# Means and roots of six routing passes made in one batch in the second attention's lead-out

## The reference

```python
x = x + _L1_ffn_ref(_layernorm(x, axis=-1), ...)

for _ in range(LOOPS):                      # LOOPS = 2
    z_norm = _rmsnorm(z, norm_w)            # mean of squares + 1e-6
    logits = z_norm @ router_w              # 8 experts
    scores = softmax(logits)
    topk_vals, topk_idx = top_k(scores, 2)  # weights normed to sum 1
    mixed = sum over experts e of cw[:, e] * ((silu(z_norm @ w1[e]) * (z_norm @ w3[e])) @ w2[e])
    z = z + mixed
```

## Time and profile before

| what | value |
|---|---|
| median of 3 runs | 2263.12 us (2262.07 to 2265.07) |
| the profiled execution | 2267.05 us, its span 2265.3 us |
| instructions | 47236 |
| mean granted clock of PE | 0.966 of full speed |

### The profile page before, as it was taken

One profiled execution on the slowest core, in us unless ns is written; L12 is line 12 of the kernel. 1 busy time (PEld: TensorE's weight loads), 2 busy tenths in 40 slices (PEclk: granted clock), 3 DMA queues, 4 the chain that ended last, 5 costly groups with the idle time before them and its releaser, 6 DMA issues. The chain is left out here.

```text
span 2265.3 us, 47236 instructions
## 1 busy us (share of the span) xinstructions
PE 2000.4 (88%) x14589; PEld 958.0 (42%) x14589; DVE 1849.5 (82%) x5293; ACT 1465.1 (65%) x3369; POOL 1235.4 (55%) x1708
## 2 busy tenths in 40 slices
PE   5999999999988999899999999985788999999992
PEld 1222222222222466444444444442455666666662
DVE  8999999999999576788888888885878787767555
ACT  1788888888888533477777777772445655565551
POOL 6343343343321012567677777744566777777776
PEclk9999999999999999799999999995889999999996
DMA  7355345345432002242333433312233444444544
GB/s 187 104 125 139 114 113 144 111 108 140 130 104 84 3 1 56 58 108 65 95 77 86 86 82 91 75 42 75 79 103 98 122 120 120 123 126 124 145 134 111
DMA packets 224626, 226.94 MB, mean 100 GB/s; under 512 B 34048, under 2 KB 187520, under 8 KB 224384
## 3 DMA queue, kind: packets, MB, share of 16 engines
q1 hardware_dynamic: 152432, 164.62, 28.0%
q0 software_dynamic: 16384, 33.59, 5.1%
q10 hardware_dynamic: 55568, 25.71, 3.9%
HBM read 96.48 MB, written 125.76 MB: 98 GB/s over the span
## 5 line engine op out<-in xcount | busy, mean ns | idle before, releaser
L899 ACT ACTIVATE big<-mid_ps 128x512 f32<-128x512 f32 (+2 forms) x1792 | 914.1, 568 | 268.5 <-PE mid_ps L778 260.7
L984 DVE TENSOR_REDUCE mid_nmax<-mid_ps 128x1 f32<-128x512 f32 (+2 forms) x1280 | 776.8, 658 | 61.3 <-PE mid_ps L757 35.5
L757 PE MATMUL mid_ps<-KT,QT 48*128 48x512 bf16 (+3 forms) x2048 | 605.1, 351 | 68.3 <-DVE mid_nmax L984 49.7
L778 PE MATMUL mid_ps<-QT,KT 64*128 64x512 bf16 (+3 forms) x2048 | 564.4, 347 | 2.7 <-ACT big L899 2.7
L794 PE MATMUL mid_ps<-big,vv 128*32 128x512 f32 (+3 forms) x4096 | 467.8, 530 | 16.7 <-POOL big L1115 12.8
L757 PEld LDWEIGHTS mid_ps<-KT,QT 48*128 48x128 bf16 x2048 | 159.1, 94 | 586.3 <-DVE mid_nmax L984 397.8
L981 DVE CUSTOM_DVE_ANT_0 big<-mid_ps,mask 128x512 bf16<-128x512 f32 (+1 forms) x512 | 304.6, 620 | 70.1 <-PE mid_ps L757 65.2
L1628 PE MATMUL moe_ps<-big,moe_xinT 128*128 x638 | 337.7, 612 | 0.0
L1773 POOL DMA_INDIRECT moe_yg<-rows_out,moe_gat_idx x256 | 251.6, 983 | 80.8 <-issue 65.8
L1759 POOL DMA_INDIRECT rows_in<-moe_xn,moe_scat_idx x240 | 236.6, 986 | 108.0 <-issue 58.9
L1690 ACT ACTIVATE moe_xinT<-moe_ps,norm_w 128x128 f32<-128x128 f32 x319 | 116.6, 366 | 226.3 <-PE moe_ps L1640 154.6
(11 more groups left out here) (328 smaller groups left out, 3047.5 us busy)
## 6 DMA issues: line engine op xcount, KB each, us to landing
l_spread<-mid_slots SPq DMA_DIRECT2D x128, 384.0 KB, 5.3
rows_in<-mid_blank SPq DMA_DIRECT2D x64, 512.0 KB, 3.7
QT<-l_spread SPq DMA_DIRECT2D x128, 192.0 KB, 4.3
KT<-l_spread SPq DMA_DIRECT2D x128, 192.0 KB, 5.3
moe_xin<-rows_in SPq DMA_DIRECT2D x319, 64.0 KB
rows_out<-moe_y ACTq DMA_DIRECT2D x319, 64.0 KB
x<-in_L_attn_x_dram SPq DMA_DIRECT2D x8, 512.0 KB, 6.5
QT<-mid_mrows SPq DMA_DIRECT2D x256, 6.0 KB
```

Of the source, the lines that this page charges most:

```text
L757: mm = pe.matmul(ps[:, bank, n_keys * a:n_keys * (a + 1)], QT[rows, par, pair, i * P:(i + 1) * P], KT[rows, par, pair, 0:n_keys], start=Tr ...
L778: mm = pe.matmul(ps[:, bank, m * a:m * (a + 1)], KT[rows, own, pair, i * P:(i + 1) * P], QT[rows, own, pair, SEQ - m:SEQ], start=True, sto ...
L899: act.activation(weights_of(r, i, heads), ps[:, ring(S2, n - 2, k), 0:widths[i] * len(heads)], ACT.Exp, scale=scale).then_inc(exp_done, 1)
L984: dve.tensor_reduce(to, of, X_AXIS, ALU.max, negate=True).then_inc(s1_used, 1)
```

## The change

`Lead.ahead` is new. It makes the statistics of x for passes 1 to 6 (48 tiles of rows, x tiles 8 to 55), their means, the first roots (`roots`) and the second roots (`scales`) in arrays of 48 columns, in four parts: part 0 (40 bn_stats) at the end of (0, 0), part 1 (8 bn_stats and the moments) at (1, 15) ahead of the wait for the router products, part 2 (first root and what leads to the second) at (2, 5), part 3 (second root) at (4, 0). It uses the centering arrays of the second attention as scratch. In the experts' block passes 1 to 6 then skip s = 0 to 3, 5 to 8 on DVE and read means, roots and scales. The passes' table is changed: `begin` of passes 2, 3, 5, 6, 7 and 8, and `length` of passes 1 to 6 is 10 and no longer 14. POOL's due times follow from them.

```diff
--- before.py
+++ after.py
@@ -408,6 +408,7 @@
         self.xn, self.z = sb("xn", [P, IT, DIM], F32), sb("z", [P, IT, DIM], F32)
         self.sel = sb("sel", [P, 2, IT, EXPERTS], F32)
         self.at, self.weight, self.scat = sb("at", [P, 2, IT], F32), sb("weight", [P, 2, IT], F32), sb("scat", [P, 2, IT], I32)
+        self.means, self.roots, self.scales = (sb(k, [P, 6 * IT], F32) for k in ("means", "roots", "scales"))
         self.run_sum, self.region, self.falling = (sb(k, [P, EXPERTS], F32) for k in ("run_sum", "region", "falling"))
         self.upper, self.ones = sb("upper", [P, P], BF16), sb("ones", [P, P], BF16)
         self.const, self.chain = sem("const"), sem("chain")
@@ -418,8 +419,9 @@
         self.sel_ready, self.k_made = sem("sel_ready"), sem("k_made")
         self.scattered = [sem(f"scattered{a}") for a in range(3)]
 
-    def place(self, big, ps, zeroed):
-
+    def place(self, big, ps, zeroed, center):
+
+        self.center = center
 
         self.zT, self.zeroed = big[:, self.ZT:self.ZT + IT * P], zeroed
         self.psT = [ps[:, a, :] for a in range(2)]
@@ -488,6 +490,36 @@
             act.activation(m["pr"], m["sh"], ACT.Exp).then_inc(self.exp_ready, 1)
             act.wait_ge(self.second_ready, 1)
             act.activation(m["e2"], m["second"], ACT.Exp).then_inc(self.e2_ready, 1)
+
+    def ahead(self, dve, part, x_added):
+
+        c, n = self.linked, 6 * IT
+        stats = self.center["stats"]
+        var, diff, tmp = (self.center[k][:, 0:n] for k in ("var", "diff", "nmean"))
+        means, roots, scales = self.means[:, :], self.roots[:, :], self.scales[:, :]
+        even, odd = stats[:, 0:n, 1], stats[:, 0:n, 4]
+        if part < 2:
+            if part == 0:
+                dve.wait_ge(x_added, BATCHES - 2)
+            for t in range(0, 5 * IT) if part == 0 else range(5 * IT, n):
+                last = dve.bn_stats(stats[:, t, :], self.x[:, IT + t, :])
+            c.link(last)
+        if part == 1:
+            dve.tensor_tensor(means, even, odd, ALU.add)
+            dve.tensor_tensor(var, stats[:, 0:n, 2], stats[:, 0:n, 5], ALU.add)
+            c.link(dve.tensor_tensor(diff, even, odd, ALU.subtract))
+            dve.tensor_scalar(means, means, 0.5, None, ALU.mult)
+            dve.tensor_scalar(var, var, 1.0 / DIM, None, ALU.mult)
+            c.link(dve.scalar_tensor_tensor(diff, diff, 0.25, diff, ALU.mult, ALU.mult))
+            c.link(dve.tensor_tensor(var, var, diff, ALU.add))
+            c.link(dve.tensor_scalar(diff, var, 1e-5, None, ALU.add))
+        if part == 2:
+            c.link(rsqrt(c, roots, diff, tmp))
+            c.link(dve.tensor_tensor(var, var, roots, ALU.mult))
+            c.link(dve.tensor_tensor(var, var, roots, ALU.mult))
+            c.link(dve.tensor_scalar(var, var, 1e-6, None, ALU.add))
+        if part == 3:
+            c.link(rsqrt(c, scales, var, tmp))
 
     def vector(self, dve, off, u, x_added):
 
@@ -532,8 +564,14 @@
             c.link(dve.tensor_scalar(var, var, 1e-6, None, ALU.add))
             c.link(rsqrt(c, rstd, var, tmp))
             dve.tensor_tensor(self.xn[:, :, :], self.z[:, :, :], each_row(rstd), ALU.mult).then_inc(self.xn_ready, 1)
+            self.ahead(dve, 0, x_added)
+        if (off, u) == (2, 5):
+            self.ahead(dve, 2, x_added)
+        if (off, u) == (4, 0):
+            self.ahead(dve, 3, x_added)
         if (off, u) == (1, 15):
             c = self.linked
+            self.ahead(dve, 1, x_added)
             dve.wait_ge(self.r_made, 1)
             c.link(dve.tensor_tensor(lg, self.psR, over(rstd), ALU.mult))
             c.link(dve.tensor_reduce(m["mx"], lg, X_AXIS, ALU.max))
@@ -1263,7 +1301,7 @@
         shared["PT"] = big
         for k, rows in (("ffn_xnT", lead_pass.xn), ("ffn_sg", lead_pass.z)):
             shared[k] = rows[:, :, :].rearrange("p (a t) d -> p a (t d)", a=2)
-        lead_pass.place(big, ps, zeroed)
+        lead_pass.place(big, ps, zeroed, center)
 
         spare, at = shared["PT"], 2 * 4 * P * TILES * (TILES + 1) // 2
         for k, n in (("qk", 2 * SEQ), ("squares", 2 * SEQ), ("gvar", P), ("grs", P), ("gtmp", P), ("aoT", SEQ), ("proj", SEQ),
@@ -1401,14 +1439,14 @@
     HT, MOST = IT * max(sizes), max(tiles_in)
     unit_of = [max(u for u in range(UNITS) if first_of[u] <= k) for k in range(LOOPS * GROUPS)]
     EARLY, PER_TILE = 2, 0.5
-    begin = {2: 0, 3: 10, 4: 22, 5: 36, 6: 49, 7: 62, 8: 78, 9: 97, 10: 117, 11: 137, 12: 158, 13: 179, 14: 200, 15: 224,
+    begin = {2: -1, 3: 8, 4: 22, 5: 34, 6: 46, 7: 60, 8: 76, 9: 97, 10: 117, 11: 137, 12: 158, 13: 179, 14: 200, 15: 224,
              16: 256, 17: 270, 18: 286, 19: 308, 20: 325}
     transfers = ("s1 s2 s3 g8 s4 s5 s6 g9 s7 g10 s8 g11 s9 g12 s10 g13 s11 g14 s12 g15 s13 g16 s14 g17 s15 g18 "
                  "g19 g20 g21 g22 g23").split()
 
     def length(k):
 
-        return 14 if k < GROUPS else 20 if k < LOOPS * GROUPS else 8
+        return 10 if k < GROUPS - 1 else 14 if k < GROUPS else 20 if k < LOOPS * GROUPS else 8
 
     def sides(n):
 
@@ -1869,6 +1907,12 @@
                         moments()
                         c.link(dve.tensor_tensor(ms[:, :], mean[:, :], mean[:, :], ALU.mult))
                         c.link(dve.scalar_tensor_tensor(var[:, :], var[:, :], 1e-6, ms[:, :], ALU.add, ALU.add))
+                elif 1 <= k < GROUPS - 1:
+                    own = slice(IT * (k - 1), IT * k)
+                    if s == 4:
+                        c.link(dve.tensor_tensor(zs, xs, each_row(lead.means[:, own]), ALU.subtract))
+                        dve.tensor_tensor(zs, zs, each_row(lead.roots[:, own]), ALU.mult).then_inc(z_ready, 1)
+                        dve.wait_ge(z_ready, k + 1)
                 else:
                     if s == 0:
                         c.link(bn(xs))
@@ -1892,18 +1936,20 @@
                 if not routes(k):
                     return
 
-                if s == 6:
+                made = 1 <= k < GROUPS - 1
+                scale = lead.scales[:, IT * (k - 1):IT * k] if made else rstd[:, :]
+                if s == 6 and not made:
                     rsqrt_seed(c, rstd[:, :], var[:, :])
                     cubic_root(c, rstd[:, :], var[:, :], tmp[:, :])
-                if s == 7:
+                if s == 7 and not made:
                     cubic_step(c, rstd[:, :], tmp[:, :])
-                if s == 8:
+                if s == 8 and not made:
                     c.link(newton(c, rstd[:, :], var[:, :], tmp[:, :]))
                 if s in (9, 10):
                     if s == 9 and k >= 3:
                         dve.wait_ge(scattered[k % 3], 16 * 2 * IT * (k // 3))
                     own = slice(IT // 2 * (s - 9), IT // 2 * (s - 8))
-                    last = dve.tensor_tensor(xn[:, k % 3, own, :], zs[:, own, :], each_row(rstd[:, own]), ALU.mult)
+                    last = dve.tensor_tensor(xn[:, k % 3, own, :], zs[:, own, :], each_row(scale[:, own]), ALU.mult)
                     if s == 10:
                         last.then_inc(xn_ready, 1)
                         dve.wait_ge(xn_ready, k + 1)
@@ -1911,7 +1957,7 @@
                 sel = sel_of(k)
                 if s == 12:
                     dve.wait_ge(r_made, k + 1)
-                    c.link(dve.tensor_tensor(lg[:, :, :], psR, over(rstd), ALU.mult))
+                    c.link(dve.tensor_tensor(lg[:, :, :], psR, over(scale), ALU.mult))
                     c.link(dve.tensor_reduce(mx[:, :], lg[:, :, :], X_AXIS, ALU.max))
                     dve.tensor_tensor(sh[:, :, :], lg[:, :, :], over(mx), ALU.subtract).then_inc(shifted, 1)
                 if s == 13:
```

## The result

The changed kernel takes 2241.1 us (median of four runs, 2239.5 to 2243.3) where the kernel before, timed beside it, takes 2263.4: a ratio of 0.9903, 95% interval 0.9891 to 0.9915. 22.4 us are gone; the forecast was 2238.1 (25 us), the range 2229 to 2252. The profiled execution took 2240.62 us with a span of 2238.8. L1913 and L1914 are the new centring of passes 1 to 6.

A forecast was written before the change was run, and what follows sets the result against it. The end is the start of POOL's unbroken run at g9, set by late tiles, plus a constant. Start 2.2, stalls 15.7 and clock 6.5 sum to 24.4, second sum 28.7; taken 25: 2263.1 - 25 = 2238.1 us, range 2229 to 2252.

The forecast's parts named there:

- The start: Experts' stage, pass 1: first scatter 4.77 us sooner; first tile, bound by its scattered rows, gains 2.2 us.
- The stalls: First loop's tiles: of PE's waits for DVE and scattered rows, up to 23.2 us open, 15.7 us go.
- rival A: First loop: shortened passes come in bursts, y copies still wait, clock drops; gain 10 to 15 us, 2251; chance 0.20.
- The clock: First loop: PE's clock at 0.91 loses 15.8 us; 6.5 us come back, bounds 0 and 13.
- The second sum: First loop's 72 tiles at the second loop's 5.6 us a pass above tile pace: 28.7 us sooner, the optimistic sum.
- DVE's work: Passes 2 to 6, beside tiles: 7.0 us a pass, 35 us in all, leave DVE.
- The lead-out: End of second attention: 16 us of added DVE work fit in 17.2 us of idle time; cost 0, bounds 0 and 2.
- Rival D: Lead-out: added operations run as slowly as L532, lead-out grows 27 us and eats the gain; 2265; chance 0.05.
- allowance for part 1: Lead-out: by the two-port blocking rule only part 1, beside POOL's selects, overflows, by under 1 us; sum 24 instead of 25.
- POOL's floor: From s1 to g9, 112 transfers take 143 to 145 us: g9 not before 1731.4; at 1740.4 POOL keeps 9 us of holes.
- rival B: POOL is the floor: tiles reach the optimistic sum or better, g9 at 1731 to 1735; gain 30 to 34 us, 2231; chance 0.10.
- rival C: Tile loop unchanged, its waits moving to ScalarE's copies, only the start moves: 2 to 5 us, 2260; chance 0.05.

The follow-up runs named there:

- the table alone: Kernel before with only the new begins and ten steps, no batch: 2273.6 us beside 2261.8, ratio 1.0044; repeated beside 2534 us: 0.9984.
- the batch alone: Changed kernel with the old begins and fourteen steps: 2248.8 us beside 2261.8, ratio 0.9944; repeated beside 2534 us: 0.9972.
- pass 1 alone: Changed kernel with the old table, only pass 1 using the batch, passes 2 to 6 making their own statistics: ratio 0.9992 beside 2534 us.
- The overfilled cover: Changed kernel with part 0 making its 40 statistics twice in the lead-out: 2247.2 us beside 2264.8, ratio 0.9926.
- the first four kernels: Against the kernel before: new table only, 0.9984; batch with old table, 0.9972; batch made but unused, old table, 1.0001; only pass 1 using it, 0.9992.
- the last: Changed kernel with ten linked products added on DVE at tile step 100: 2513.7 us beside 2533, ratio 0.9925.
- the four timed beside 2264.8 us: Changed kernel with part 0's statistics doubled, 2247.2 us; pass 3 two steps later, 2243.8; pass 7 four earlier, scatters before g9, 2248.3; both table edits, 2250.2.

## Why the prediction was right, step by step

*What bounds the kernel.* That the end is the start of POOL's unbroken run plus a constant held: g9 came 24.5 us sooner and the span is 26.5 us shorter, the second-loop stretch kept its length, and POOL held for 6.1 us made the rest of the span 6.5 us longer and the kernel 7.4. From g9 to the end of the span there are 499.9 us before, 500.2 with the table alone, 498.6 with the batch alone and 497.9 in the changed kernel, and behind g9 POOL never stands longer than 0.8 us in any of the four.

*The start.* Forecast 2.2 us, measured 2.2 from the iota to the first tile, and pass 1 alone shows it (2.2 to 2.6). The row that was said to bound it did: the first tile waits for its rows, 5.3 us after POOL's last lead scatter (1578.84 to 1584.18) where 4.9 were taken from a later pass. The first scatter came at 1584.47, 22.0 us after the iota against 26.8 before: 4.8 us, as priced.

*The stalls.* Forecast 15.7 us gone of 23.2 open; measured some 10: PE's idle time from the first to the 72nd tile is 19.9 us against 30.2 before. Here the term was too large: 1.5 us a pass were left standing, but the y copies alone still cost 7.4 us. Of the 28.1 us of waits that the sum counted, for DVE and for scattered rows, 16.3 are left (7.4, 4.6 and 3.0, and 1.3 for pass 7's centring), so 11.8 went. And a wait came that the trace of before does not have, for ScalarE's copy of the transposed rows (5.2 us, five times). It comes with the ten steps: the table alone has it (5.3 us), the batch with the old table has it not. Where passes 2 and 3 are pressed together one tile comes 9.2 us after the last, 7.6 over the pace; this is rival A's mechanism, in small.

*The clock.* Forecast 6.5 us of 15.8 back; measured 0.91 of 175.8 us against 0.96 of 156.3 us, so 15.8 us lost before and 6.3 after: 9.5 back by the forecast's own reckoning, part of it inside the waits. PE's busy time holds no waits and fell by 9.2 us for the same 72 tiles. Where PE stood less the mean clock was higher; what made it fall each time was not looked for. Idle and busy together, 10.2 and 9.2, are the 19.5 us of the stretch, where 22.2 were forecast. The two terms missed in opposite directions, the stalls by 5.5 too much and the clock by 2.7 too little, so that the sum is closer than its terms is in part luck. The second sum (28.7 us) was too hopeful: a pass still costs (156.3 - 117.4) / 5.9 = 6.6 us above the pace, not 5.6 (5.9 passes and no longer 5.7, since pass 7 begins two steps sooner). It was 10.2.

*DVE's work.* 29.7 us left the stretch (144.55 to 114.90), where 35 were priced. In part this is the price: the 7.0 us of a pass were read as elapsed time, with the gaps of linked operations in them. In part it is the stretch, which now holds more of pass 7. The term did not enter the sum but through the waits.

*The lead-out.* Forecast 0, measured 0 within what the traces can tell, and the forecast durations held: 7.8 us for 40 statistics (8.2 forecast), 1.64 for eight. The overfilled cover shows that this was no luck of a hidden slack. Rival D had no part: linked operations of 48 columns took 0.18 to 0.25 us, so that no operation of the batch shows a lengthening of the kind of the old L532. The eight statistics beside POOL's select of 1542.59 took 1.64 us, 0.205 each, against 7.82 / 40 = 0.196 for those beside an idle POOL. The prediction had put its allowance for part 1 down to the Trainium skill (SBUF — State Buffer, "Who interferes with whom"), but that section also says that a DVE instruction with at most one SBUF input, outside the two-port modes, does not contend with GpSimd, and a statistics instruction has one input. It says too that one with two SBUF inputs contends with a GpSimd instruction that reads SBUF. The trace agrees on both: the lead pass's own L395, with two inputs, took 0.54 us beside the select of 1546.80 and 0.23 us at 1548.85 with no select beside it.

*POOL's floor.* 1584.47 + 144 = 1728.5 was the earliest for g9; it came at 1740.86, 12 us over it (9 forecast). That the tiles still set it shows in the releaser before g8 and g9, the results of the tiles written to memory. So rival B was not reached; rival C fell with the 19.5 us.

What the prediction did not separate is which half of the change carries it. It took the table for a detail of size (1.5 us a pass); the runs show that the table is worth 8 to 9 us with the batch and costs 10 to 12 without it.

## What to carry to other kernels

Work moved out of a crowded loop pays in full only when the schedule behind it is moved too: here the lighter passes alone brought 13 of 22 us and left an engine's queue waiting for indices that a fixed step delivered late, and the tighter schedule alone made the kernel slower. So try the halves of such a change apart only to understand it, not to judge it. When one in-order queue runs without a hole to the end, forecast the moment at which that run starts; and when you price what a relieved engine gives back, read its busy time and not the elapsed time of a linked chain, and count with new short waits where passes are pressed together.

## What was not expected of the hardware

Beside the first four kernels the kernel before took 2534 us and beside the last 2533, where it takes 2262 to 2265 elsewhere, with a mean granted clock of 0.93 instead of 0.97. In the traces of those four the experts' stage begins at 1562.1 to 1563.4 us, as in the others, so the 270 us lie in that stage. There POOL stands in holes of 3 to 23 us almost to the end, and in one of 41 to 44 us near it, instead of running without one. The instructions themselves are not slower: in the two traces of the kernel with the batch alone, at 2525 and at 2249 us, ACT's copy of a tile's transposed rows takes 368 and 366 ns and a POOL scatter 0.98 us. What is added is idle time, much of it such as the trace ties to no instruction of this core: from 1760 to 2240 ACT stands 107 us in 21 such pieces, of up to 8.6 us, before that copy, and has none of them in the faster trace. The cause was not looked for. That it lies in the chip is not shown either, for the record gives the same chip number to these four kernels and to the four timed beside 2264.8 us. A part of a gain can vanish there (the batch alone: 0.9972 instead of 0.9944).
